# Group norm, per-channel shift and 3x3 blur on one core: looped ScalarE and VectorE programs, and the sums of a whole unit ahead of the variances of the unit before

## The reference

```python
def _gn(v, G=32, eps=1e-5):             # group norm: 32 groups of 24 channels
    g = v.reshape(B_, G, C_ // G, H_, W_)
    m = jnp.mean(g, axis=(2, 3, 4), keepdims=True)
    s = jnp.var(g, axis=(2, 3, 4), keepdims=True)
    return ((g - m) / jnp.sqrt(s + eps)).reshape(v.shape)
...
off_px = offset * 64; off_int = round(off_px); sub = off_px - off_int   # one offset per 16 channels
shifted = x moved by off_int pixels, zero outside the image
kern = 3x3 Gaussian (sigma 0.5) centred at sub, normed to sum 1
out = depthwise 3x3 convolution of shifted with kern, padding SAME
...
x = x + _L0_conv_ref(_gn(x), L0_conv_offset)
```

## Time and profile before

| | |
|---|---|
| median of 3 runs | 1246.45 us (1244.77 to 1249.37) |
| the profiled execution | 1247.67 us, span 1245.5 us |
| mean granted TensorE clock | 0.829 |
| busy: PE, DVE, ACT, POOL | 860.3, 836.2, 649.8, 354.7 us |
| DMA | 403.30 MB, mean 324 GB/s |

### The profile page before, as it was taken

The page is one execution under the profiler, slowest core; times in us unless marked ns, Lnnn a source line. Parts: engine busy times, 40 slices in busy tenths (PEclk is TensorE's granted clock), DMA queues, the critical chain, the costliest instruction groups (busy, mean ns, idle before and its releaser), DMA issues.

```text
span 1245.5 us, 9666 instructions
## 1 busy us (share of the span) xinstructions
PE 860.3 (69%) x2176; PEld 417.6 (34%) x2176; DVE 836.2 (67%) x580; ACT 649.8 (52%) x514; POOL 354.7 (28%) x598
## 2 busy tenths in 40 slices
PE   2976775768676596657867768877968576886710
PEld 1433332334333243323433334333433332443310
DVE  5287496866848668584874957576776758557584
ACT  0464355544557644665455556544545565555561
POOL 5024232233321324312332321322233213222121
PEclk9997877978888797878978888887988788787855
DMA  9527969797997887889699997989998896998635
GB/s 383 226 106 294 384 227 407 285 386 314 337 403 298 325 349 274 363 289 399 236 374 372 348 401 283 401 343 381 372 352 332 326 411 250 401 349 310 283 135 245
DMA packets 46269, 403.30 MB, mean 324 GB/s; under 512 B 21648, under 2 KB 21648, under 8 KB 21648
## 3 DMA queue, kind: packets, MB, share of 16 engines
q0 software_dynamic: 30720, 201.40, 42.6%
q1 hardware_dynamic: 15504, 201.39, 39.9%
HBM read 201.38 MB, written 201.33 MB: 323 GB/s over the span
## 4 chain that ended last, share of the span: by engine, by line
DVE 26%; PE 20%; DMA 14%; ACT 12%; issue 10%; POOL 9%; ACTq 6%; DVEq 2%; POOLq 0%
PE sum_ps L273 16%; DMA xs<-x_dram 12%; ACT frame L344 6%; DVE smooth L519 6%; DVE smooth L516 6%; ACTq L329 5%; DVE xs L523 5%; DVE xs L526 5%; ACT unused L371 4%; DVE xs L529 3%; POOL small L233 3%; DMA out_dram<-xs 2%; POOL small L235 2%; DVEq L536 1%; POOL small L237 1%
## 5 line engine op out<-in xcount | busy, mean ns | idle before, releaser
L273 PE MATMUL sum_ps<-xs,bands 128*128 128x512 f32 x1024 | 511.9, 658 | 42.2 <-DVEq L425 22.1
L371 ACT ACTIVATE unused<-xs,small 128x4096 bf16<-128x4096 f32 x96 | 356.1, 3709 | 53.6 <-issue 51.3
L516 DVE SCALAR_TENSOR_TENSOR smooth<-frame,xs 128x1700 f32 (+5 forms) x96 | 163.5, 1703 | 308.7 <-ACT frame L351 217.2
L273 PE MATMUL sum_ps<-xs,halves 128*128 128x512 f32 x512 | 250.5, 646 | 98.5 <-DMA xs<-x_dram 98.4
L273 PEld LDWEIGHTS sum_ps<-xs,bands 128*128 128x128 f32 x1024 | 212.2, 213 | 292.6 <-issue 270.5
L344 ACT ACTIVATE frame<-xs,small (+1 forms) x96 | 222.8, 2321 | 63.6 <-DVE smooth L519 63.3
L523 DVE SCALAR_TENSOR_TENSOR xs<-smooth,small,xs 128x1700 f32 (+5 forms) x96 | 163.5, 1704 | 65.2 <-POOL small L245 62.9
L273 PEld LDWEIGHTS sum_ps<-xs,halves 128*128 128x128 f32 x512 | 104.8, 209 | 242.0 <-issue 242.0
L519 DVE SCALAR_TENSOR_TENSOR smooth<-frame,xs,smooth 128x1700 f32<-128x1700 f32 (+5 forms) x96 | 163.6, 1704 | 3.4
L526 DVE SCALAR_TENSOR_TENSOR xs<-smooth,small,xs 128x594 f32 (+9 forms) x96 | 159.8, 1664 | 3.4
L529 DVE SCALAR_TENSOR_TENSOR xs<-smooth,small,xs 128x594 f32 (+9 forms) x96 | 159.7, 1664 | 3.4
(11 more groups left out here) (85 smaller groups left out, 394.1 us busy)
## 6 DMA issues: line engine op xcount, KB each, us to landing
xs<-x_dram SPq DMA_DIRECT2D x96, 1024.0 KB, 11.1
xs<-x_dram POOLq DMA_DIRECT2D x192, 512.0 KB, 12.0
out_dram<-xs SPq DMA_DIRECT2D x96, 1024.0 KB, 8.8
out_dram<-xs POOLq DMA_DIRECT2D x192, 512.0 KB, 10.6
smooth<-offset_dram SPq DMA_DIRECT2D x1, 48.0 KB, 3.5
```

The costliest lines, as they stand in the source:

```text
L273: last = nc.tensor.matmul(sum_ps[u % 2][:, :], (FIRST, SAME, SECOND)[i], slot_px(n, c * BANK, (c + 1) * BANK), start=(i == 0 and c == 0), ...
L371: nc.scalar.activation(unused[:, :], slot_px(n), ACT.Square, bias=neg_mean[:, u % 2, i:i + 1], accum_out=squares[:, u % 2, i:i + 1]).then_ ...
L516: V.scalar_tensor_tensor(sm, frame_window(-1), side_w[:, bass.ds(n, 1), 0], frame_window(0), ALU.mult, ALU.add).wait_op(frame_ready, done_ ...
```

## The change

What it does, engine by engine:

- TensorE: the sums of all three tiles of unit u+1 stand ahead of `variances(u)`; before, those of the third tile stood behind. There is one PSUM bank for the sums in place of two. The seven variance matmuls are the same in number, sorted by the square that they wait for.
- ScalarE: the program is a loop over units (`Fori`) with three fills in its body. The fill of a tile reads one packed word and not four. `means(u + 1)` and the first square come before the second fill, one square stands between any two fills, and the means are copied once more (`fill_mean`).
- VectorE: one loop over tiles in place of two nested ones, one packed word and not three.
- GpSimd: the nine first loads are issued after the small memsets and the selection and no longer ahead of them.

```diff
-            def sum_tile(u, i):
...
+            def sums(u):
+                if u:
+                    pe.wait_ge(mean_sum_ready, u)
+                for i in range(UT):
+                    n = u * UT + i
+                    pe.wait_ge(loaded[n % SLOTS], 16 * (n // SLOTS + 1))
+                    pe.wait_ge(outer_loaded[n % SLOTS], 32 * (n // SLOTS + 1))
+                    for c in range(CHUNKS):
...
+                last.then_inc(sums_ready, 1)
...
             for u in range(UNITS):
+
                 if u + 1 < UNITS:
-                    sum_tile(u + 1, 0)
-                    sum_tile(u + 1, 1)
+                    sums(u + 1)
                 variances(u)
                 if u + 1 < UNITS:
-                    sum_tile(u + 1, 2)
                     means(u + 1)
...
+            def means_to_fill(u):
+                nc.scalar.activation(fill_mean, neg_mean, ACT.Copy).then_inc(fill_mean_ready, 1)
+                act.wait_ge(fill_mean_ready, u + 1)
...
+            def unit_of(u, ahead=True):
+
+                fill_frame(u, 0)
+                next_fill(u, 0)
+                variances(u)
+                if ahead:
+                    sum_means(u + 1)
+                    means(u + 1)
+                    square(u + 1, 0)
+                fill_frame(u, 1)
+                next_fill(u, 1)
+                if ahead:
+                    square(u + 1, 1)
+                fill_frame(u, 2)
+                if ahead:
+                    next_fill(u, 2)
+                    means_to_fill(u + 1)
+                    square(u + 1, 2)
...
-            for u in range(UNITS):
-                ahead = u + 1 < UNITS
-                fill_frame(u * UT)
-                variances(u)
-                if ahead:
-                    sum_means(u + 1)
-                fill_frame(u * UT + 1)
-                if ahead:
-                    means(u + 1)
-                    square(u + 1, 0)
-                fill_frame(u * UT + 2)
-                if ahead:
-                    square(u + 1, 1)
-                    square(u + 1, 2)
...
+            with act.Fori(1, UNITS - 1) as u:
+                unit_of(u)
...
-                for register, word in ((kind_at, KIND), (to_pixel, DST), (from_pixel, SRC)):
-                    dve.reg_load(register, table[0:1, bass.ds(n, 1), word:word + 1])
...
+                dve.reg_load(entry, windows[0:1, bass.ds(n, 1)])
...
-            with dve.Fori(0, UNITS) as unit:
-                with dve.Fori(0, UT) as i:
-                    tile_of(unit, i)
+            with dve.Fori(0, TILES) as n:
+                tile_of(n)
```

More of the change, by code:

```diff
@@ L218, in _ @@
                             pattern=[[-1, SET], [-SET, P // SET]], channel_multiplier=1).then_inc(pool_ready, 1)
+            for n in range(SLOTS):
+                load(n)
             V.memset(zeros, 0.0)
@@ L288, in variances @@
+                nc.tensor.matmul(mean_ps[:, 2:3], OF_SECOND, mean_sum, start=True, stop=True).then_inc(mean_ps_ready, 1)
             def variances(u):
-                first, middle, last = (squares[:, u % 2, i:i + 1] for i in range(UT))
-                pe.wait_ge(squares_ready, UT * (u + 1))
+                first, middle, last = (squares[:, i:i + 1] for i in range(UT))
                 if u >= 1:
                     pe.wait_ge(var_ready, u)
-                nc.tensor.matmul(var_ps[:, 0:1], ALL, first, start=True, stop=False)
@@ L303, in _ @@
-            for i in range(UT):
-                sum_tile(0, i)
+                pe.wait_ge(squares_ready, UT * u + 1)
+                nc.tensor.matmul(var_ps[:, 0, 0:1], ALL, first, start=True, stop=False)
+                nc.tensor.matmul(var_ps[:, 1, 0:1], FIRST, first, start=True, stop=False)
+                pe.wait_ge(squares_ready, UT * u + 2)
+                nc.tensor.matmul(var_ps[:, 0, 0:1], OF_FIRST, middle, start=False, stop=True)
+                nc.tensor.matmul(var_ps[:, 1, 0:1], SAME, middle, start=False, stop=False)
@@ L305, in _ @@
+                nc.tensor.matmul(var_ps[:, 2, 0:1], OF_SECOND, middle, start=True, stop=False)
+                pe.wait_ge(squares_ready, UT * u + 3)
+                nc.tensor.matmul(var_ps[:, 1, 0:1], SECOND, last, start=False, stop=True)
+                nc.tensor.matmul(var_ps[:, 2, 0:1], ALL, last, start=False, stop=True).then_inc(var_ps_ready, 1)
+            sums(0)
             means(0)
@@ L341, in emit @@
                     b = target.with_bounds(min_val=PAD * PITCH, max_val=(PAD + H - rows) * PITCH)
[L342 to L343 removed]
+                    if not first:
+                        act.wait_ge(smooth_ready, done)
                     nc.scalar.activation(
@@ L500, in _, with smooth_tile @@
             done_count = dve.alloc_register("done_count")
-            def smooth_tile(rows, cols, src, dst, n, done, unit, weights):
+            def smooth_tile(rows, cols, src, dst, n, done, weights):
                 around = frame[:, bass.ds(src - 1, rows * PITCH + 2)]
```

178 lines of the change are left out of this document (87 added, 91 removed).

## The result

The changed kernel takes 1333.42 us (median of 4 runs, 1331.68 to 1337.26) against 1247.58 us before (median of 4): a ratio of 1.0694 with a 95% interval of 1.0662 to 1.0727. That is 86 us slower; 49 us were forecast, and the time lies above the range. The profiled execution has a span of 1331.9 us at a mean granted clock of 0.81.

What follows compares the result with a forecast made beforehand. It took a chain of waits through the third tile's landing, 75.6 us a pair of units, as the bound. 1247.7 - 8 - 4 + 79 = 1314.7, less 18 relief and 1.2 from profile to median: 1295.5 us, range 1258 to 1322.

Steps and rivals of the forecast that it cites:

- The new wait: TensorE: variances stand behind the next unit's third-tile sums, making them and the weights 10.2 us later in unit 8.
- 10 us and not 5: Sign to look for in the new trace: the time from the end of the sums to the second fill.
- I take back 1.2 us a pair, 18 in all: Saturated DMA round of store and load: a kernel idling 5 us more a pair has fewer transfers queued, -18 us.
- 1313: Rival without relief: the DMA round stays as it is, about 1313 us, chance 0.33.
- +79 us: Summed loss over even units 2 to 30 from later weights and second fills, variance-reading savings already taken off.
- The second link: GpSimd's next third-tile load stands behind late weights and first tile; after unit 6, unit 7's variances at 342.3, against 340.4.
- The start, "-8": Kernel start: with memsets ahead of GpSimd's loads, TensorE's first sums end near 37.5 and not 45.6 us.
- The end, "-4": Last unit: nothing hides VectorE's saved gaps of about 2 us, two of them, and some of ScalarE's: -4 us.
- The square ahead of the second fill: ScalarE: variances, means and a 3.71 us square before the second fill make it 7.1 us later.
- The loops: Looped ScalarE and VectorE programs: a real gain by the instruction fetch page, but off the chain by the rows.

Runs made afterwards that it cites:

- gate_alone: The kernel before, with only TensorE's sums of the next unit's third tile moved ahead of the variances: 1334.67 us, ratio 1.0731.
- fewer_bytes: The changed kernel, with SyncE storing only a quarter of the pixels of the middle 64 partitions for odd (small-window) units: 1226.18 us, ratio 0.983.
- start_alone: The kernel before, with GpSimd's first loads issued behind the small memsets and the selection: 1239.83 us, ratio 0.9963.
- old_act_order: The changed kernel with ScalarE's old order: second fill straight behind the sums, one and two squares between fills; TensorE's new order stays: 1329.82 us, ratio 1.0671.
- loops_alone: The changed kernel with TensorE's and ScalarE's old orders back; looped programs, packed words, one PSUM bank and new start stay: 1215.46 us, ratio 0.975.

## Why the prediction was wrong, point by point

- **The new wait was the right mechanism.** Variances behind the third tile's sums, VectorE waiting for weights in the even units, the second fill 7 us later behind the sums: all of it is in the trace (for the fill, the "10 us and not 5" of the signs is 7.7 and not 0.7, and 12.0 and not 4.8 to VectorE's start), and `gate_alone` shows that this one edit makes the loss.
- **"I take back 1.2 us a pair, 18 in all" failed.** There is no relief. From the weights to the third tile's landing it was 29.7 us before and 29.9 after on average in even units, and in odd ones 22.6 and 22.1. I reasoned that a kernel that idles more has fewer transfers queued. But the idle time came after the landing, at a share of 0.27, while the same burst of bytes was queued after the end of the large unit. `fewer_bytes` shows that this stretch follows the bytes. This step is half of the miss, and without it the forecast was 1313, still below what was measured.
- **"+79 us" was too small: +90.** From the weights of unit 1 to those of unit 31 (the units 2 to 30 of the sum) the changed kernel falls from 2.5 us ahead to 87.5 behind. Pair by pair, units 4, 6, 18 and 20 gave 33 us (34 forecast), units 2, 8 and 10 gave 22 (22), and unit 30 gave -2.5 (-2); the 11 us lie in units 12, 14, 22 and 24 with 23 (16), 26 and 28 with 7 (3), and 16 with 7.8 (6). For the first four of these I had let only the sums' 7 us move ahead and taken part of that off again. On average over the even units the variances leave TensorE 10.2 us after the third tile's landing, where they left 0.2 us ahead of it, and the weights end 2.7 us behind them, where it was 5.8. In that 10.2 I had 8.7, with sums of 7.1 us; they took 8.6.
- **The second link** is in the trace in every odd unit: their variances leave TensorE 10.3 us after the landing of the next third tile. But it adds nothing. From the weights of an even unit to those of the odd one behind it, it was 38.2 us before and 37.3 after; the whole loss is in the other round, 35.3 before and 42.9 after.
- **The start, "-8", was right by itself and worth 2.5 in this kernel.** `start_alone` keeps its 8 us. I did not carry the new wait back to unit 0, whose variances now wait for three tiles that TensorE sums one after the other until 60.8 us.
- **The end, "-4":** 87.5 behind at the weights of unit 31 and 86.4 at the end of the span, so -1.1.
- **The square ahead of the second fill:** its 7 us are in place, but under another wait. `old_act_order` is within noise of the changed kernel. Where the new wait is taken away it counts in nearly all pairs, 66 us, which I had not seen: I had let it act in the pairs with a small first tile alone.
- **The loops.** I had them off the chain. `loops_alone` is 32 us faster than the kernel before by the medians and 29 by the spans: its weights are 7 us ahead at unit 1, 20 at unit 29 and 28 at unit 31. So 7 are the start and 13 come in between, and the last units and the end, where I had 4, gave 9. What in the edit gives the 13 was not taken apart: the loops, the packed words, the one PSUM bank and the variance matmuls sorted by square are all in it. VectorE's gaps without a releaser shrank only from 81.2 to 60.4 us there and did not go. ScalarE's 78.3 us before L364, up to 4.6 us each, are 20.7 us there and 1.2 at most, and q14 brings 12 instruction packets and no longer 28. By the Trainium skill ("Runtime: NRT & Kernel Launch", instruction fetch mechanics) a taken branch out of the two blocks of instructions that an engine holds stalls for a fetch. ScalarE's rows agree with that, but do not show it, since the same edit took three register loads from each fill; for VectorE no run here shows what its remaining gaps are.
- **What the sum gives with the measured terms:** 1245.5 (span) - 2.5 + 90.0 - 1.1 = 1331.9, the span after. Against the forecast the relief makes 18 us of the miss, the even units 11, the start 5.5 and the end 3.

`fewer_bytes` gains more (107 us) than its 37.7 MB take at 407 GB/s (93 us, or 5.8 a pair). Over units 4 to 29 a pair is 7.7 us shorter: 6.8 in the stretch to the landing, and 1.0 from the landing to the variances, where the sums were shorter. Why the stretch gains 6.8 and not 5.8 stays open, and so does what the granted clock costs the kernel as a whole.

## What to carry to other kernels

Work put ahead of a small result in an in-order engine's program makes that result wait for everything that the work waits for, so ask of each such wait when its data lands, and follow it round the loop until it meets itself, in the first iterations too: here one line moved past seven small matmuls cost 7%. When a stall lengthens a cycle that has a saturated DMA stretch in it, credit nothing to less crowded transfers unless the bytes in that stretch change; the idle time may fall elsewhere. Time the edits of a change apart, since a gain of 32 us lay hidden under this loss.

## What the runs showed of the hardware

- At a share of 1.0 the DMA moved 396 to 409 GB/s in the stretches shown, whatever the order of issue. Issuing a store 5.0 us earlier into such a stretch brought the tile behind it 1.1 us earlier on average (33.8 and 35.0 us from the end of the large unit).
- From the reading of the variances to the end of GpSimd's six small operations it took 2.7 us on average in the even units of the changed kernel, where VectorE stood idle, and 4.4 in those of the kernel before, where it was 2.6 to 7.1 us as VectorE's passes ran beside them or not.
- The third tile's 16 passes took 7.1 us at a granted clock of 1.00, and 10.14 us in unit 8 of the changed kernel, where TensorE had stood for 5.88 us before them. The granted clock over those 10 us was 0.69 of the higher level, 2.4 GHz, so a part of them ran at the lower, 1.2 GHz.
